# The skip term of a state-space mixer: from TensorE's products with a diagonal matrix to a map on GpSimd and an addition on VectorE

## The reference

```
x = x + layernorm(mixer(layernorm(x)))
x = x + layernorm(ffn(layernorm(x)))

mixer(h): h + mamba(rmsnorm(h))
  z, xbc, dt = split(u @ in_proj.T)            # 512, 2560, 8 columns
  xbc = silu(causal convolution of 4 taps over tokens)
  X (8 heads x 64), B, C (8 heads x 128) = split(xbc)
  dt = softplus(dt + bias); a = -exp(A_log) * dt; cum = cumsum(a) in chunks of 128 tokens
  Y_intra[l] = sum_s (C[l] . B[s]) exp(cum[l] - cum[s]) [s <= l] dt[s] X[s]
  Y_inter[l] = exp(cum[l]) C[l] H              # H: state at the chunk's start
  H = exp(cum[last]) H + sum_s B[s] exp(cum[last] - cum[s]) dt[s] X[s]
  y = Y_intra + Y_inter + D_skip[head] * X     # the last product is the skip term
  y = rmsnorm(y * silu(z)) @ out_proj.T
ffn(h): silu(h @ W_up.T) @ W_down.T + experts(h)
  experts: two searches over 64 keys for each of 4 heads, the 8 best sums of 8 x 8,
  softmax, weights on 1024 experts, silu(h @ down_embed.T * weights) @ up_embed
```

## Time and profile before

| | |
|---|---|
| median of 3 runs | 2614.18 us |
| the profiled execution | 2616.56 us, of which span 2614.8 us |
| TensorE matmuls busy | 2521.9 us (96%) |
| TensorE weight loads busy | 2004.5 us (77%) |
| GpSimd busy | 2168.8 us (83%) |
| VectorE busy | 2120.7 us (81%) |
| ScalarE busy | 1824.3 us (70%) |
| mean granted TensorE clock | 0.991 |

### The profile page before, as it was taken

The page is one execution under the profiler, slowest core; times in us unless marked ns, Lnnn a source line. Parts: engine busy times, 40 slices in busy tenths (PEclk is TensorE's granted clock), DMA queues, the critical chain, the costliest instruction groups (busy, mean ns, idle before and its releaser), DMA issues. The chain is left out here.

```text
span 2614.8 us, 58427 instructions
## 1 busy us (share of the span) xinstructions
PE 2521.9 (96%) x18552; PEld 2004.5 (77%) x18616; DVE 2120.7 (81%) x5397; ACT 1824.3 (70%) x3745; POOL 2168.8 (83%) x3130
## 2 busy tenths in 40 slices
PE   5899999999999999999999999999999999999987
PEld 4677877877877878777778777778777778778766
DVE  5688888878888878888878888878888888888877
ACT  4577777677777677777777777767777767776754
POOL 4488888888888888888888888888888888888875
PEclk8999999999999999999999999999999999999999
DMA  4000000000000000000000000000000000000000
GB/s 144 9 9 14 6 12 8 12 12 12 4 8 12 12 12 12 4 8 12 12 12 12 4 8 12 12 12 12 4 8 12 12 12 5 11 8 12 9 5 9
DMA packets 28861, 34.33 MB, mean 13 GB/s; under 512 B 2704, under 2 KB 27280, under 8 KB 28240
## 3 DMA queue, kind: packets, MB, share of 16 engines
q1 hardware_dynamic: 28816, 33.77, 4.1%
HBM read 25.37 MB, written 8.39 MB: 13 GB/s over the span
## 5 line engine op out<-in xcount | busy, mean ns | idle before, releaser
L1221 DVE SCALAR_TENSOR_TENSOR acc<-bank,cw,acc 128x253 f32<-128x253 f32 x1920 | 770.3, 472 | 102.3 <-ACT acc L858 102.3
L1618 PE MATMUL bank<-hT,w_in 128*128 128x256 f32 x2560 | 618.4, 385 | 13.8 <-DVE acc L1221 11.3
L1618 PEld LDWEIGHTS bank<-hT,w_in 128*128 128x128 f32 x2560 | 480.5, 192 | 129.7 <-issue 38.5
L645 POOL TENSOR_TENSOR Em<-ee 128x1024 f32<-128x1024 f32 x256 | 490.4, 1926 | 11.1 <-DVE rden L1357 6.3
L1377 DVE SCALAR_TENSOR_TENSOR Em<-Em,p 128x1024 f32<-128x1024 f32 x256 | 354.0, 1413 | 85.3 <-POOL Em L645 85.3
L660 POOL TENSOR_TENSOR W<-W,Em 128x1024 f32<-128x1024 f32 x124 | 295.0, 2379 | 51.4 <-ACT Em L993 43.5
L858 ACT ACTIVATE acc<-bank,cb,cw 128x253 f32<-128x253 f32 x640 | 324.0, 559 | 0.0
L993 ACT ACTIVATE Em<-Em,rden 128x1024 f32<-128x1024 f32 x256 | 289.9, 1145 | 47.4 <-DVE Em L1387 45.6
L1387 DVE TENSOR_TENSOR Em<-Em,products 128x1024 f32<-128x1024 f32 x248 | 297.3, 1210 | 0.0
L1810 PE MATMUL bank<-h2T,w_up 128*128 128x256 f32 x1024 | 244.8, 382 | 2.1 <-ACT hid L971 1.4
L1844 PE MATMUL bank<-w_ue,WT 128*128 128x256 f32 x1024 | 234.1, 382 | 0.2 <-ACT WT L1003 0.2
(11 more groups left out here) (210 smaller groups left out, 5013.1 us busy)
## 6 DMA issues: line engine op xcount, KB each, us to landing
x_in<-x_dram SPq DMA_DIRECT2D x32, 256.0 KB, 2.7
x_res<-x_dram SPq DMA_DIRECT2D x32, 256.0 KB, 2.7
out_dram<-f SPq DMA_DIRECT2D x32, 256.0 KB, 2.2
w_in<-in_wT_dram SPq DMA_DIRECT2D x1, 1544.0 KB, 8.8
w_in<-in_wT_dram SPq DMA_DIRECT2D x1, 1024.0 KB, 5.3
w_up<-upT_dram SPq DMA_DIRECT2D x1, 1024.0 KB, 13.2
w_de<-down_eT_dram SPq DMA_DIRECT2D x1, 1024.0 KB, 15.2
w_down<-downT_dram SPq DMA_DIRECT2D x1, 1024.0 KB, 17.5
```

What stands on the lines that cost most here:

```text
L645: nc.gpsimd.tensor_tensor(Em[:, k], bc(ee[:, k, 0:XD], 2, KEYS), bc(ee[:, k, XD:XD + KEYS], 1, XD), ALU.mult).then_inc(E_done.sem, 1)
L1221: ins = V.scalar_tensor_tensor(acc[:, r, a, TAPS - 1:], ps[:, a * TOK + k:(a + 1) * TOK - TAPS + 1 + k], cw[:, t, k:k + 1], acc[:, r, a, T ...
L1618: last = mm(ring[j % 2][:, a * TOK:(a + 1) * TOK], w_in[:, k, at:at + P], hT[:, k, :], start=k == 0, stop=k == DK - 1)
```

## The change

TensorE's four skip products, the matrix `skip` and the function `skip_weights` go. GpSimd makes `DX` = D_skip times `Xt` for each chunk (`mixer_DX`), and VectorE adds it to `yv` (`mixer_skip`) between `mixer_state` and `mixer_gate`. ScalarE's `mixer_move` waits for `DX_done` before it overwrites `Xt`. The products of `sL` and `Xdt` start their sums themselves. In `mixer_cum` the two 128x16 products are issued in pieces of 32 columns of the weights. The orders of GpSimd, VectorE and ScalarE in `do_group` are changed, and those of all four engines in `ending`; TensorE's order in `do_group` stays. The diff, cut to what is spoken of:

```diff
-            def skip_weights():
-                for i in range(INNER // P):
-                    nc.gpsimd.tensor_tensor(skip[:, 2 * i:2 * i + 2], ident[:].rearrange("p (h d) -> p h d", h=2),
-                                            bc(head_c[:, 2, 2 * i:2 * i + 2], 2, HD), ALU.mult).then_inc(skips, 1)
-
             def mixer_norm(g):
 
 
...
 
+            def mixer_DX(g, c):
+                pool.wait_ge(X_sb.sem, X_sb.at(g, c))
+                if c or later(g):
+                    pool.wait_ge(skip_added.sem, skip_added.at(g, c - 1))
+                nc.gpsimd.tensor_tensor(heads3(DX[:]), heads3(Xt[:]), bc(head_c[:, 2, :], 2, HD), ALU.mult)\
+                    .then_inc(DX_done.sem, 1)
+
             def mixer_decay(g, c):
...
             def do_group(g, e, f, n):
                 a, b, c = g is not None, e is not None, f is not None
 
+                if c:
+                    weigh(f, 0, 3)
                 if b:
                     mixer_root_y(e)
-                    mixer_decay(e, 1)
-                if c:
+                if c:
+                    weigh(f, 1, 0)
                     collect(f, 0, 1)
-                    weigh(f, 1, 0)
-                    collect(f, 0, 2)
                 if b:
                     tail_root3(e)
+                if c:
+                    weigh(f, 1, 1, 2)
                 if a:
                     mixer_dt_abs(g)
                 if c:
-                    weigh(f, 1, 1)
+                    weigh(f, 1, 3)
                 if b:
                     tail_root4(e)
-                if c:
-                    weigh(f, 1, 2, 3)
                 if a:
                     mixer_dt(g)
                 if c:
-                    collect(f, 0, 3)
+                    collect(f, 0, 2, 3)
                 if b:
                     ffn_args(e, 0)
+                if c:
+                    collect(f, 1, 1, 2)
                 if a:
                     mixer_keep(g)
                 if c:
-                    collect(f, 1, 1, 2)
+                    collect(f, 1, 3)
+                if a:
+                    mixer_cum(g)
                 if b:
                     ffn_args(e, 1)
-                if c:
-                    collect(f, 1, 3)
-                if a:
-                    mixer_cum(g)
+                if a:
                     mixer_parts(g)
                 if n is not None:
                     mixer_norm(n)
                 if a:
                     mixer_head(g)
                 if b:
-                    weigh(e, 0, 0)
+                    weigh(e, 0, 0, 1)
+                if a:
+                    mixer_decay(g, 0)
+                    mixer_scale(g, 0)
+                if b:
                     pool.wait_ge(rden_done.sem, rden_done.at(e))
                 if c:
                     ffn_root(f)
                 if b:
-                    weigh(e, 0, 1)
-                if a:
-                    mixer_scale(g, 0)
-                    mixer_decay(g, 0)
-                if b:
-                    weigh(e, 0, 2, 3)
-                if a:
-                    mixer_scale(g, 1)
+                    weigh(e, 0, 2)
+                if a:
+                    mixer_DX(g, 0)
                 if n is not None:
                     mixer_halo(n)
+                if a:
+                    mixer_DX(g, 1)
+                    mixer_scale(g, 1)
+                    mixer_decay(g, 1)
                 pool.wait_ge(own_pool, own.n)
...
                     act.wait_ge(Xw_done.sem, Xw_done.at(g, c - 1))
+                    act.wait_ge(DX_done.sem, DX_done.at(g, c - 1))
                 nc.scalar.activation(Xt[:], ring[c][:], ACT.Copy).then_inc(X_sb.sem, 1)
 
...
             def do_group(g, e, f, n):
                 a, b, c = g is not None, e is not None, f is not None
 
-                if b:
-                    mixer_square(e, 1)
                 if c:
                     tail_keep(f)
-                if b:
-                    mixer_yT(e, 1)
+                    ffn_experts(f, 0, 1)
+                if a:
+                    mixer_pair(g, 0)
                 if c:
                     ffn_experts(f, 0, 2)
                 if a:
-                    mixer_pair(g, 0)
                     mixer_pair(g, 1)
                     mixer_dt(g)
-                    mixer_dt_exp(g)
-                    mixer_u(g)
                     silu(g, 0)
                     mixer_pair(g, 2)
-                if c:
-                    ffn_experts(f, 0, 3)
-                if a:
+                    mixer_dt_exp(g)
                     silu(g, 1)
                     mixer_pair(g, 3)
                 if b:
                     tail_norm(e, g)
+                if c:
+                    ffn_experts(f, 0, 3)
                 if a:
                     mixer_z(g, 0)
                 if b:
                     mixer_z(g, 1)
                 if a and not later(g):
                     search_weights()
+                if a:
+                    mixer_u(g)
                 if b:
                     ffn_sim(e, 0)
+                if c:
+                    ffn_experts(f, 1, 0)
                 if a:
                     silu(g, 2)
                     mixer_pair(g, 4)
-                if c:
-                    ffn_experts(f, 1, 0)
                 if b:
                     ffn_sim(e, 1)
                 if a:
...
                     mixer_pair(g, 5)
                 if b:
                     ffn_up(e, 0)
+                if c:
+                    ffn_experts(f, 1, 1)
                 if a:
                     silu(g, 4)
                     mixer_pair(g, 6)
                 if c:
-                    ffn_experts(f, 1, 1)
+                    ffn_WT(f, 0)
+                    ffn_experts(f, 1, 2)
                 if b:
                     ffn_up(e, 1)
-                if c:
-                    ffn_WT(f, 0)
                 if a:
                     silu(g, 5)
                     mixer_pair(g, 7)
                 if c:
-                    ffn_experts(f, 1, 2)
+                    ffn_experts(f, 1, 3)
                 if a:
                     silu(g, 6)
                     mixer_pair(g, 8)
-                if c:
-                    ffn_experts(f, 1, 3)
-                if a:
                     mixer_cum(g)
                     silu(g, 7)
                     mixer_pair(g, 9)
                 if b:
                     ffn_up(e, 2)
+                    ffn_exp(e)
+                if a:
+                    mixer_exp(g)
                 if c:
                     ffn_WT(f, 1)
-                if b:
-                    ffn_exp(e)
                 if a:
                     silu(g, PAIRS - 2)
+                if b:
+                    ffn_up(e, 3)
+                if a:
+                    silu_head(g)
                 if n is not None:
                     mixer_norm(n, e)
                 if a:
-                    silu_head(g)
-                if b:
-                    ffn_up(e, 3)
-                if a:
                     silu(g, PAIRS - 1)
+                    mixer_move(g, 0)
                 if n is not None:
                     mixer_hT(n)
                 if a:
-                    mixer_exp(g)
-                    mixer_move(g, 0)
                     mixer_decay(g, 0)
                     mixer_B(g, 0)
+                    mixer_decay(g, 1)
+                    mixer_move(g, 1)
                 if c:
                     ffn_norm(f)
                 if a:
-                    mixer_decay(g, 1)
                     mixer_B(g, 1)
-                    mixer_move(g, 1)
+                    mixer_yT(g, 0)
                     mixer_square(g, 0)
-                if b:
-                    ffn_experts(e, 0, 0, 1)
-                if a:
-                    mixer_yT(g, 0)
+                    mixer_yT(g, 1)
+                    mixer_square(g, 1)
+                if b:
+                    ffn_experts(e, 0, 0)
 
             mixer_norm(0, None)
             mixer_hT(0)
...
 
+            def mixer_skip(g, c):
+                dve.wait_ge(Yi_read.sem, Yi_read.at(g, c))
+                dve.wait_ge(DX_done.sem, DX_done.at(g, c))
+                V.tensor_tensor(yv[:, c], yv[:, c], DX[:], ALU.add).then_inc(skip_added.sem, 1)
+
             def mixer_step(g, c):
                 dve.wait_ge(H_scaled.sem, H_scaled.at(g, c))
                 dve.wait_ge(S_ps.sem, S_ps.at(g, c))
                 V.tensor_tensor(H[:], H[:], ring[c][:], ALU.add).then_inc(H_done.sem, 1)
 
             def mixer_gate(g, c):
-                dve.wait_ge(Yi_read.sem, Yi_read.at(g, c))
+                dve.wait_ge(skip_added.sem, skip_added.at(g, c))
                 dve.wait_ge(Yn_ps.sem, Yn_ps.at(g, c))
                 V.tensor_tensor(yv[:, c], yv[:, c], yb[:], ALU.add).then_inc(Yn_read.sem, 1)
...
 
                 if b:
                     mixer_gate(e, 1)
+                    mixer_step(e, 1)
                 if c:
                     ffn_mask(f, 0, 2, 3)
                     ffn_times(f, 0, 2)
```

(55 more changed lines are left out.)

76 lines of the change are left out of this document (37 added, 39 removed).

## The result

The changed kernel takes 2681.32 us (median of 4 runs, 2679.83 to 2682.38), the kernel before 2615.33 on the same chip (4 runs, 2614.05 to 2617.98): ratio 1.0251, 95% interval 1.0233 to 1.0268. The forecast was 2714, range 2575 to 2745. The direction held, and the forecast collisions occurred; but the loss is 66 us, not 100, and a part of it came from moves that the prediction had priced at nothing. The profiled execution took 2682.38 us, its span 2680.6 (before 2614.8).

The account below looks back on a forecast made before the run. TensorE was taken as the bound, with GpSimd's chain becoming it after the change. 29 groups x 3.45 us = 100 us, other terms 0, took the profiled 2616.6 to 2717, so 2714 by the median; range 2575 to 2745.

Parts of the forecast that it names:

- Products removed, and where the gain goes: TensorE's skip products: 2.08 us a group removed, pieces save 0.15; before other waits worth only 0.4 to 0.8 a group.
- Work added: Per chunk, DX on GpSimd 1.04 us and the addition on VectorE 0.69; 2.1 and 1.4 us a group.
- The collisions: VectorE instructions reading two SBUF tensors and GpSimd's long ones exclude each other for a whole instruction, through shared ports.
- The walk: GpSimd's new order followed through one group: second DX ends at 71.9 us, group at 83.0 instead of 78.96, +4.0.
- first pass: An earlier walk of the group with GpSimd's dt at 14.5 us: group ends at 81.8, +2.9 us.
- near today's 49.4 either way: TensorE's start with cum_parts: asked for at 48.1 us, but ScalarE's WT copies, behind the exponentials, last till 49.2.
- The sum: Whole kernel: 29 groups x 3.45 us = 100 us slower; groups 0 to 2 and the ending 0.
- The signs: Profile marks of a right forecast: period near 82.4 us, GpSimd busy above 72, chunk 1's addition 1.3 to 1.7.
- Moves that cost nothing: Reordered times ahead of conv(4), mixer_u, residual and ScalarE's table load: no loss expected; the times free 2.3 us.
- The gain stays: Rival: DX and addition find gaps, TensorE keeps 2.23 us a group, 2543 us; chance 0.18.
- No blocking: Rival: GpSimd and VectorE stay apart, group ends by 78.4 us, -15 us in all, 2600; chance 0.15.
- Nothing moves: Rival: half of the collisions, last Em product ends before the gate; group 78.7 to 79.2, 2605 to 2621; chance 0.05.

Follow-up runs that it names:

- orders alone: The changed kernel with its new orders, loops and ending, but the skip term back on TensorE (no DX, no addition): 2651.22 us, ratio 1.0129.
- skip move alone: The kernel before with its old orders, only the skip term moved to GpSimd maps and VectorE additions: 2637.98 us, ratio 1.0078.
- no skip term: The kernel before with the skip term left out, no products on TensorE and nothing in their place: 2596.12 us, ratio 0.9926.
- isolated pairs: A program of its own without the computation, pairing one VectorE and one GpSimd instruction: the two-tensor addition takes 0.68 us alone, 2.67 beside GpSimd's product.

## Why the prediction was right, and where its size was off

*Products removed, and where the gain goes.* Right: 0.62 us a group measured, 0.4 to 0.8 forecast. In the orders of before this term decided the sign: map and addition cost 1.25 us there, less than the 2.08 that the products' length promised. One reading of a row was off without effect: chunk 0's products stand 6.1 us ahead of chunk 1's, not 7. The `cum` pieces save 0.11 (0.15 forecast), by the start of the last of them 0.25 us behind the first instead of 0.36; a wait takes it back.

*Work added.* Right: 1.04 and 0.69 us where nothing holds them.

*The collisions.* Right as a mechanism: shown in isolation, and in the changed kernel by the addition of chunk 1 (1.44 against 0.73 us) and the gate's product.

*The walk.* Three points of TensorE, counted from the group's start, medians of 25 groups; "rows" is the first product with `cum_parts`:

| | rows | `Yn` of chunk 1 | next group |
|---|---|---|---|
| before | 49.4 | 72.3 | 78.96 |
| forecast | 49.2 to 49.4 | 74.9 | 83.0 (81.8 in the first pass) |
| changed | 50.4 | 73.5 | 80.96 |
| orders alone | 50.5 | 73.1 | 79.79 |
| skip move alone | 49.4 | 72.1 | 79.59 |
| no skip term | 49.4 | 71.6 | 78.34 |

Up to the rows GpSimd's walk was good: `dt` at 15.8 (16.1 forecast), `cum_parts` done at 49.2 (49.3). But TensorE starts the rows at 50.4: I had `WT` ready by 49.2. In fact `ffn_up(e, 2)` starts at 44.8 (before 44.3), behind a wait of 0.2 us for a sum of `W` and this one, which is TensorE's:

```profile
1252.25 1.99 PE L1625 MATMUL bank<-hT,w_in 128*128 128x256 f32 x8 [0.18 <-DVE acc L1224]
1254.08 1.89 PE L1815 MATMUL bank<-h2T,w_up 128*128 128x256 f32 x8
```

and ScalarE's chain behind it starts at 47.35 and gives the first half of `WT` at 50.1:

```profile
1256.62 1.28 ACT L983 ACT_TABLE_LOAD   x1
1257.92 0.84 ACT L983 ACTIVATE ee<-ee 128x768 f32<-128x768 f32 x1
1258.67 0.23 ACT L883 ACTIVATE ecum<-cum 128x48 f32<-128x48 f32 x1
1258.80 1.06 ACT L1010 ACTIVATE WT<-bank 128x512 f32<-128x512 f32 x2
```

So "near today's 49.4 either way" failed by 1.0 us. The kernel with the orders alone is 1.06 us late there too, gets 0.2 back by the transposes of X, and keeps 0.85 from `C H` to the group's end: that is its whole +0.83. Of the 1.06, 0.63 are there at `ffn_up(e, 2)` already; that the order of ScalarE's `WT` and exponentials makes the rest is read from the timelines, no run tests it. The second `DX` ends at 70.6 (71.9 forecast), which is the first part of the mis-sized term, 1.3 us. I had added a blocked time to each neighbour in that stretch; that some fell on the same instructions is my reading, no run separates them. The gate's product was forecast done at 79.0 and is at 76.95; it was ready at 75.5, not 77, and the moved `Em` product ended at 76.4, not 78.3. From `Yn` to the end the changed kernel needs 7.4 us against 6.7, where I had 8.1.

*The sum.* The mis-sized term is "3.45 us a group": 2.00 was measured in 28 groups and 4.5 in the last, 40 us less in all. Both passes of the walk were too long (2.9 and 4.0): 1.3 us too much up to the second `DX`, 0.7 from `Yn` to the end. The ending was put at 0 with bounds of 6 and measured +5.6, just inside them; this term was too low.

*What was luck.* The prediction held the new orders to be harmless and put the whole loss on the map, the addition and what they block. The orders alone lose 36 us, and the changed kernel is only 30 us slower than that. So the forecast of a loss didn't rest on a full account of it: as far as the two can be told apart, a part put at nothing (36 us) and a part put much too high (100 us, where 30 were left) made up for each other in the sum.

*The signs.* The chunk 1 addition (1.44 us), GpSimd's longest idle time before `root_y` (2.70), `sL` without a wait for TensorE, and TensorE's 1.74 us before `Yn` came as named. Three sizes did not: the period is 80.96, not near 82.4, GpSimd is busy in 71.4 us a group, not above 72, and the wait before `yT` is 0.65 us, not 1 or more.

*Moves that cost nothing.* Wrong for the two `times` ahead of `conv(4)` and for what stands behind them. VectorE's mask `cmask` lasts 0.195 us in each of 32 groups before, and 2.24 in the median of the changed kernel, by source line:

```profile
L1323 DVE TENSOR_SCALAR cmask<-i8b x32: 195/195/197, 120.2 to 2557.9; 128x64 f32<-128x64 bf16 x32
```

```profile
L1331 DVE TENSOR_SCALAR cmask<-i8b x32: 195/2239/2250, 118.8 to 2622.0; 128x64 f32<-128x64 bf16 x32
```

Most of the 2.3 us that the moved `times` free for the convolution are spent there; TensorE is left with 0.18 us of wait. What this mask costs the changed kernel was not run. By the timelines a larger part came from a move that the prediction had also put at no loss, ScalarE's `WT` behind the exponentials.

*The rivals.* "The gain stays" fell with the kernel without a skip term: even a free skip term gives 2596 in the orders of before, and the changed orders are slower by themselves. "No blocking" fell with the isolated pairs. "Nothing moves" asked for half of the collisions; those of the second addition and of the gate's product both occurred.

## What to carry to other kernels

Before work is moved off the bound engine, leave it out in one run: that is about the most the move can win with the other orders as they are, here 19 us of a counted 67. Run a change of order without the move as well: here it lost 36 us by itself. Look at what the removed work covered. Then ask of each added instruction whether its kind excludes the other engine's for its whole length, and count it for both. Idle time of an engine off the path may be what keeps a neighbour on time; look at which instructions of the other engine run in it before it is filled.

## What the runs showed of the hardware

- The block depends on the kind. VectorE's addition of two SBUF tensors (0.68 us) is held back by GpSimd's products and maps (2.67 and 1.37) and not by a memset; its one-tensor form (0.42) by a memset too (0.99); with an operand in PSUM by none (0.68). GpSimd's instruction, when it starts first, is not slowed (2.34 beside all kinds and alone).
- I had looked only at long two-tensor instructions. Casts and masks of 64 columns are held back as well, 0.20 to 2.24 or 2.31 us, and the trace books it as busy time of the held engine.
- A wait that is cut on one engine can cost more than it was worth: some 0.35 us of TensorE's idle time ahead of the rows (0.57 in the trace) removed, 1.41 us a group lost (period 80.37 against 78.96).
